# Decoder kernel on one core: later groups' input chain, units, state sums and gated stage under other slots

## What is computed

```python
x = x + _L0_attn_ref(_layernorm(x), ...)            # selective scan
x = x + _L0_xattn_ref(_layernorm(x), ctx_1024, ...) # gated attention over the context, 4 heads
x = x + _L0_ffn_ref(_layernorm(x), ...)             # graph of 6 attention nodes, 8 heads
```

```python
dt = jax.nn.softplus(dt @ dt_proj_w.T + dt_proj_b)
dA = jnp.exp(dt[..., None] * A)
dBu = (dt * u)[..., None] * Bm[:, :, None, :]
def step(h, inp):
    dA_t, dBu_t = inp
    h = dA_t * h + dBu_t
    return (h, h)
y = jnp.einsum('lbin,bln->bli', h_seq, Cm)
y = (y + u * D) * jax.nn.silu(gate)
return y @ out_proj_w.T
```

```python
for c in range(6):
    q = ew[c, 0] * (nodes[in_q] @ We[eq] + be[eq])   # k, v alike from older nodes
    o = _mha(q, k, v, Wq[c], Wk[c], Wv[c], Wo[c])
    nodes[c] = act_w[c] * o + q
```

## Time and profile before

| what | before |
| --- | --- |
| median of 3 runs | 1204.73 us (1203.15 to 1206.0) |
| the profiled execution's own time | 1206.4 us |
| its span (first to last instruction) | 1204.5 us |
| PE matmul busy | 1092.0 us, 91% |
| PE weight loads busy | 840.4 us, 70% |
| DVE busy | 979.9 us, 81% |
| ACT busy | 733.6 us, 61% |
| start of the node graph of group 0 | 194.8 us |

### The profile page before, as it was taken

The page is one execution under the profiler, slowest core; times in us unless marked ns, Lnnn a source line. Parts: engine busy times, 40 slices in busy tenths (PEclk is TensorE's granted clock), DMA queues, the critical chain, the costliest instruction groups (busy, mean ns, idle before and its releaser), DMA issues.

```text
span 1204.5 us, 26893 instructions
## 1 busy us (share of the span) xinstructions
PE 1092.0 (91%) x11428; PEld 840.4 (70%) x11428; DVE 979.9 (81%) x1220; ACT 733.6 (61%) x1728; POOL 15.3 (1%) x33
## 2 busy tenths in 40 slices
PE   8777899999899999999899989999999988998886
PEld 6555577767676777777776767777777766776775
DVE  3799887999989989999899988998998989635122
ACT  4446444776487657766677648765776656544443
POOL 5000000000000000000000000000000000000000
PEclk9778668999999999999999989999999999999998
DMA  7732631041112211041204111221104110000000
GB/s 219 232 114 71 210 106 53 7 136 36 36 37 53 90 45 63 11 133 36 71 7 137 36 31 43 62 81 46 53 11 132 37 62 2 2 1 10 2 2 10
DMA packets 48695, 76.08 MB, mean 63 GB/s; under 512 B 5504, under 2 KB 33408, under 8 KB 48576
## 3 DMA queue, kind: packets, MB, share of 16 engines
q1 hardware_dynamic: 47872, 73.81, 19.4%
q0 software_dynamic: 704, 0.56, 0.2%
HBM read 62.55 MB, written 10.75 MB: 61 GB/s over the span
## 4 chain that ended last, share of the span: by engine, by line
PE 59%; DVE 14%; ACT 7%; issue 5%; DVEq 0%; ACTq 0%
PE ps L651 7%; PE heads L661 6%; PE ps L729 6%; PE heads L682 4%; PE ps L722 4%; PE ps L632 4%; PE heads L690 4%; PE ps L556 4%; DVE ring L1112 3%; DVE mx L1215 3%; PE ps L518 3%; PE ps L579 2%; PE heads L632 1%; PE ps L707 1%; ACT qT L934 1%
## 5 line engine op out<-in xcount | busy, mean ns | idle before, releaser
L1112 DVE TENSOR_TENSOR_SCAN ring<-dec,ring 128x1024 f32<-128x1024 f32 x128 | 292.3, 2283 | 1.0 <-ACT dec L879 0.9
L879 ACT ACTIVATE dec<-dts,a_neg 128x254 f32<-128x254 f32 x512 | 220.3, 501 | 9.9 <-DVE ring L1112 9.8
L1215 DVE TENSOR_REDUCE mx<-heads 128x16 f32<-128x2048 f32 x48 | 109.8, 2288 | 62.9 <-PE heads L682 62.3
L1121 DVE TENSOR_TENSOR ring<-ring,cs 128x1024 f32<-128x1024 f32 x128 | 156.2, 1220 | 2.0
L1105 DVE TENSOR_TENSOR ring<-dtus,bs 128x1024 f32<-128x1024 f32 x128 | 155.4, 1219 | 0.8 <-DVE fb L1026 0.5
L954 ACT ACTIVATE pr<-heads 128x512 f32<-128x512 f32 x192 | 99.1, 602 | 41.9 <-PE heads L695 41.9
L556 PE MATMUL ps<-ring,fold 128*32 128x256 f32 x1024 | 87.7, 412 | 18.6 <-DVE ring L1121 18.3
L729 PE MATMUL ps<-aT,wo_f 128*128 128x256 f32 x384 | 95.0, 388 | 8.2 <-DVE aT L1224 7.9
L722 PE MATMUL ps<-node,we_f 128*128 128x256 f32 x384 | 98.1, 401 | 0.0
L651 PE MATMUL ps<-node,wq_f 128*128 128x256 f32 x384 | 94.9, 390 | 3.4 <-ACT node L969 3.4
L661 PE MATMUL heads<-wv_f,node 128*128 128x256 f32 x384 | 93.3, 386 | 0.0
(11 more groups left out here) (191 smaller groups left out, 1755.2 us busy)
## 6 DMA issues: line engine op xcount, KB each, us to landing
dts<-dt_rows SPq DMA_DIRECT2D x31, 512.0 KB, 4.2
dtus<-dt_rows SPq DMA_DIRECT2D x31, 512.0 KB, 5.1
node<-in_w_edgeT SPq DMA_DIRECT2D x18, 256.0 KB, 3.5
bs<-bc_rows SPq DMA_DIRECT2D x32, 128.0 KB, 4.8
cs<-bc_rows SPq DMA_DIRECT2D x32, 128.0 KB, 4.8
dt_rows<-dt SPq DMA_DIRECT2D x32, 128.0 KB, 2.4
dt_rows<-th SPq DMA_DIRECT2D x32, 128.0 KB, 2.5
xin<-in_x SPq DMA_DIRECT2D x8, 256.0 KB, 3.2
```

The costliest lines, as they stand in the source:

```text
L879: last = fn(dec[k % 2][:, blk, :, 1:L], dts[c % 2][:, blk, :].rearrange("p (b t) -> p b t", b=GB)[:, :, 1:L], ACT.Exp, scale=a_neg[:, c, b ...
L1112: v.tensor_tensor_scan(states, dec[k % 2][:].rearrange("p k b t -> p (k b t)"), states, 0.0, ALU.mult, ALU.add).then_inc(sig["state"], 1)
L1121: v.tensor_tensor(states[:], states[:], cs[:, q:q + 1, :].broadcast_to([P, BLKS, T]), ALU.mult).then_inc(sig["outflow"], 1)
L1215: v.tensor_reduce(mx[:].rearrange("p (h s) -> p h s", h=HPC)[:, :, 0:STEPS], heads[:].rearrange("p h (s k) -> p h s k", s=STEPS), AX.X, AL ...
```

## The change

Every instruction stays. The tables of slots of groups 1 to 7 are others for the input chain, the units and the gated stage, the sums (`add`) leave the unit table for a table of their own, and group 0's steps keep their slots.

```diff
-    if _k >= 1:
-        U_STEPS += [("u", "add", _k - 1)]
-        if _k % CUNITS == 0:
-            U_STEPS += [("u", "gather", _k // CUNITS - 1)]
-U_STEPS += [("u", "weigh", UNITS - 1), ("u", "add", UNITS - 1), ("u", "gather", IC - 1)]
+    if _k >= 1 and _k % CUNITS == 0:
+        U_STEPS += [("u", "gather", _k // CUNITS - 1)]
+U_STEPS += [("u", "weigh", UNITS - 1), ("u", "gather", IC - 1)]
+ADD_STEPS = [("u", "add", k) for k in range(UNITS)]
...
-A_AT = [-101, -70, -68, -67, -65, -64, -62, -59, -56, -45, -42]
...
+A_AT = [-101, -69.5, -68.75, -66.5, -64.5, -63.5, -60.5, -58.25, -55.25, -44.75, -40.75]
...
+ADD_AT = [-25, -23, -16.5, -14, -4, -1.75, 2.75, 9, 10.5, 13, 20, 22.5, 24.75, 28.5, 33.25, 35.25]
...
+X_AT = [34, 37.5, 41.75, 42.75, 45.75, 47.75, 49.5, 51, 54.5, 55.25, 56.75, 57, 57.25, 60.5, 63, 64.75]
...
+FIRST = ((A_STEPS, A0_AT), (U_STEPS, U0_AT), (ADD_STEPS, ADD0_AT), (X0_STEPS, X0_AT))
+LATER = ((A_STEPS, A_AT, A_SH), (U_STEPS, U_AT, U_SH), (ADD_STEPS, ADD_AT, ADD_SH), (X_STEPS, X_AT, X_SH))
```

More of the change, by code:

```diff
@@ L97 @@
 P_STEPS = [("p", "prep", n) for n in range(3 * NODES)]
-A_AT = [-101, -70, -68, -67, -65, -64, -62, -59, -56, -45, -42]
-U_AT = [-44, -40, -40, -39, -34, -34, -32, -32, -32, -32, -32, -32, -32, -29, -29, -29, -25, -25, -25, -25, -24,
[4 rows of a table removed]
-X_AT = [26, 37, 41, 42, 45, 47, 48, 50, 54, 55, 56, 57, 57, 58, 63, 64]
+A0_AT = [-886.25, -822.5, -822, -810.25, -810.25, -810, -804.75, -803.75, -731, -617.25, -601.25]
+A_AT = [-101, -69.5, -68.75, -66.5, -64.5, -63.5, -60.5, -58.25, -55.25, -44.75, -40.75]
+A_SH = [0, -8.25, 1.75, 2, 2, 2, 2, 2]
@@ new lines @@
+U0_AT = [-122, -118, -118, -117, -112, -112, -110, -110, -110, -110, -110, -110, -110, -107, -107, -107, -103,
[4 rows of a table added]
+U_AT = [-42.5, -35.75, -35.25, -35.25, -35.25, -35.25, -32, -31.75, -31.75, -31.75, -31.75, -29.5, -29.25, -28,
[5 rows of a table added]
+U_SH = [0, 1, 1, 1, 1, 1, 1, 1]
+ADD0_AT = [-103, -101, -95, -92, -82, -80, -76, -72, -68, -65, -62, -56, -53, -50, -45, -43]
+ADD_AT = [-25, -23, -16.5, -14, -4, -1.75, 2.75, 9, 10.5, 13, 20, 22.5, 24.75, 28.5, 33.25, 35.25]
+ADD_SH = [0, 1, 1, 1, 1, 1, 1, 1]
+X0_AT = [-38.75, -30.5, -27.5, -22.5, -22, -17.25, -16.75, -16.25, -14, -14, -11, -9.75, -9, -9, -5, -3]
@@ L106 @@
+X_AT = [34, 37.5, 41.75, 42.75, 45.75, 47.75, 49.5, 51, 54.5, 55.25, 56.75, 57, 57.25, 60.5, 63, 64.75]
+X_SH = [0, 1, 1, 1, 1, 1, 1, 1]
 P_AT = [-602.5, -580.75, -567.25, -85.5, -80.75, -78.75, -63.5, -60.75, -57.5, -46.25, -34.5, -31.25, -22.5,
         -20.75, -17.5, -7.25, -2.5, -1]
[L110 to L114, removed]
@@ L115 @@
-AT = (("a", A_STEPS, A_AT, A_SH), ("u", U_STEPS, U_AT, U_SH), ("x", X_STEPS, X_AT, X_SH))
-ORDER = [(FSLOTS * g + n, 0, g, n, step) for g in range(NG) for n, step in enumerate(F_STEPS)]
[L118 to L121, removed]
@@ L122 @@
-ORDER += [(at, 3, 0, n, step) for n, (step, at) in enumerate(zip(X0_STEPS, X0_AT))]
-ORDER += [(at, 4, 0, n, step) for n, (step, at) in enumerate(zip(P_STEPS, P_AT))]
+FIRST = ((A_STEPS, A0_AT), (U_STEPS, U0_AT), (ADD_STEPS, ADD0_AT), (X0_STEPS, X0_AT))
+LATER = ((A_STEPS, A_AT, A_SH), (U_STEPS, U_AT, U_SH), (ADD_STEPS, ADD_AT, ADD_SH), (X_STEPS, X_AT, X_SH))
+ORDER = [(FSLOTS * g + n, 0, g, n, step) for g in range(NG) for n, step in enumerate(F_STEPS)]
+for _rank, (_steps, _at) in enumerate(FIRST):
+    ORDER += [(at, 1 + 2 * _rank, 0, n, step) for n, (step, at) in enumerate(zip(_steps, _at))]
@@ L125 @@
+for _rank, (_steps, _at, _shift) in enumerate(LATER):
+    ORDER += [(FSLOTS * (g - 1) + at + _shift[g], 2 + 2 * _rank, g, n, step)
+              for g in range(1, NG) for n, (step, at) in enumerate(zip(_steps, _at))]
+ORDER += [(at, 9, 0, n, step) for n, (step, at) in enumerate(zip(P_STEPS, P_AT))]
 WARM_FIRST = 10
@@ L128 @@
         -540.25, -537.5, -537.5, -537.5, -524.5, -523, -517, -517, -511.25, -508.25, -508.25, -508.25]
-ORDER += [(at, 5, 0, n, step) for n, (step, at) in enumerate(zip(W_STEPS, W_AT))]
+ORDER += [(at, 10, 0, n, step) for n, (step, at) in enumerate(zip(W_STEPS, W_AT))]
 ORDER = [(step, g) for _, _, g, _, step in sorted(ORDER)]
```

## The result

The changed kernel takes 1191.55 us as the median of 4 runs (1188.22 to 1192.87), the kernel before beside it 1203.94 (4 runs, 1200.33 to 1206.0). The ratio is 0.9896, with a 95% interval of 0.9877 to 0.9914: 12.4 us faster. Five more runs of the changed kernel gave 1191.28, ratio 0.9901 (0.9881 to 0.9922). The forecast was 1199.4, 5.3 us faster, with a range of 1195.3 to 1205.5.

A forecast was written before the change was run, and what follows sets the result against it. Neither TensorE nor VectorE alone was taken as the bound; only changed waits count. Six graphs at -0.79 (-4.7), graph ends -1.7 and group 6 +1.1 gave -5.3, from 1204.73 to 1199.4 us, range 1195.3 to 1205.5.

The forecast's parts named there:

- Node 0, +0.27: Node 0: with the gather between the halves of `aT`, the second half reaches TensorE's output 0.27 us late.
- Start of node 2, +0.43 on TensorE: Node 2's start: decays ahead of `qT` must wait for the scan, so `qT` and TensorE are 0.43 us later.
- Subtraction of node 2: Node 2: `mxT` freed from the decay pair gives -0.79 against +0.43 at the start; the scan replaces VectorE's idle free.
- Transposes -0.49: Context transposes leave the place ahead of node 2's edge product and fit TensorE's 0.66 wait before node 3's scores: -0.49 us.
- halves -0.31: Node 2's output: both halves of `aT` ahead of the weighing remove TensorE's 0.31 us wait before L729's second half.
- First rival: VectorE sets the period and only its gaps count: -0.58 us a graph, 1202.3 in all; chance 0.16.
- End of a graph, -0.34: Graph ends: the sum ahead of the input chain's transposes fills their 0.34 us wait for ScalarE; five graphs, -1.7.
- Graph 6, +1.1: Graph 6: -0.6 in node 0, +2.2 for node 2's uncovered scan, -0.49 for context transposes; together +1.1 us.
- Node 4, +0.10: Node 4: the values' copy ahead of four decays shifts ScalarE's idle before the node's copy; taken as +0.10 us.
- The clock: Rival: gaps gathered in one place bring one more low-clock stretch a graph, 8.6 us, 1208.0, slower; chance 0.08.
- a small gain for one fewer: Larger-gain case: group 3's second low-clock stretch goes (-1.4) and node 0 costs nothing (-1.6): 1196.4; chance 0.10.

The follow-up runs named there:

- gather_back: The changed kernel with node 0's gather ahead of both halves of the product again; median 1190.02 us, ratio 0.9886.
- before_fill: The kernel before with eight unread matmuls ahead of TensorE's wait for the last head's values in node 5; 1201.64 us, ratio 0.9986.
- best: The changed kernel with node 0's gather ahead of both halves for groups 1 to 6, and group 7's maximum ahead of node 2's scan; 1182.26 us, ratio 0.9829.

## Why the prediction was wrong

**Node 0, +0.27: right in sign, measured +0.41.** The second half of `aT` waits behind the gather and nothing brings that back (`gather_back`). VectorE's idle ahead of the first half is 1.62, not 2.0.

**Start of node 2, +0.43 on TensorE: wrong.** The decays did wait for the scan (0.52 of idle) and `qT` is 0.40 later. But the copy of dt had started 0.95 behind `qT`, at 505.32 against 504.37, and now starts 0.71 behind it (370.31, 371.02), which takes up 0.24 of that:

```profile
505.32 0.84 ACT L847 ACTIVATE dt<-ps,vec 128x256 f32<-128x256 f32 x2
```

TensorE's wait grew from 1.01 to 1.17 only.

**Subtraction of node 2: -0.36 forecast, -0.51 measured.** The scan found its cover in groups 0 to 5, as forecast, and had none in graph 6 (+2.17 against 2.2).

**Transposes -0.49 and halves -0.31: the step that failed.** I took each wait of TensorE for a cost of its own. From node 2's maximum to node 3's, VectorE works in graphs 0 to 4 with no other waits than 0.14 and 0.51 in the layer norm, which the change leaves, so those waits of TensorE were only VectorE's delay seen from TensorE. The two edits alone gave +0.32 and +0.07. What the change gained there is VectorE's idle of 1.49, and to that the forecast gave nothing: the scan and the idle were to change places at no cost, and the gain stopped at the subtraction. Over both pieces -1.52 was measured and my sum had -1.16. That the two are near each other is luck: -0.80 of the -1.16 are two terms that don't hold, and the idle was left out.

**First rival.** Its mechanism held in node 2 of graphs 0 to 4 and failed as a rule for the period. Its -1.49 stands against the measured -1.52; the 0.29 that it added between the halves of node 2 didn't come in the change. Its sum of -0.58 a graph assumed that VectorE sets the other nodes too: it had +0.62 in node 0, where +0.41 was measured, and nothing for the end of a graph, where TensorE's order gave -0.73. The Trainium skill, "Perfetto Trace Analysis", "Identifying the Most-Contended Engine", which points to VectorE by its occupancy, agrees with the trace in that stretch, where the time follows VectorE's idle; the shares of the whole window (93% and 72%) could not say in which stretch.

**End of a graph, -0.34: mis-sized, -0.73 measured.** The sum's own move brought 0.46, since it closed VectorE's 0.33 ahead of node 0's maximum too, and for the other 0.27 I had missed the projection between keys and queries.

**Graph 6, +1.1: right,** +1.3 measured, and in its terms too: -0.44 for node 0 (-0.6), +2.17 for the scan (+2.2), -0.39 behind it (-0.49). **Node 4, +0.10:** -0.06.

Of the miss of 0.77 in each of graphs 0 to 4, node 2 makes 0.36, the end of the graph 0.39, node 4 0.16, and node 0 0.14 the other way. By graphs: five graphs at -1.90 and not -1.13 make 3.9 of the miss, graph 5 (-1.39, not -0.79) 0.6, the other way 0.2 in graph 6. That is 4.3 of 7.1 us. The rest, 2.8, is in no term. The profiles show nothing else that differs than the clock and the first part; how the 2.8 divides between them isn't shown.

**The clock.** As a rival I had only more stretches, and a small gain for one fewer. The profile had 9, and I took the profiled execution as typical. At 1206.4 it is 3.5 over the later median of 23 runs (1202.86) and above the slowest of them (1206.34), so fewer stretches were more likely than more.

**Still open.** Why the same wait of 1.36 is followed by a stretch in graph 2 of the change and not in graph 1; and why the first part ends between 208.7 and 211.9 in kernels with the same order there. Every piece was read from one profiled execution of its kernel; that they repeat within 0.02 us from graph to graph is what they rest on.

## What to carry to other kernels

Before adding up the waits of one engine, look whether another works almost without a gap across the same stretch. If it does, its own gaps are the sum and the first engine's waits are one delay, seen several times; an edit that fills one of them then gives nothing, or takes cover away elsewhere. Ask it graph by graph: here graph 5 answered otherwise than graphs 0 to 4. And one profiled execution is one draw: count its low-clock stretches, and compare kernels by distances between fixed points in pieces that have none.

## What the runs showed of the hardware

A wait of 1.36 us of TensorE (573.03 in the earlier trace rows), in a graph of 130.29 us in which its matmuls are busy for 122.44, can be followed by 3.41 us at the granted clock 0.50, its level of 1.2 GHz. Such a stretch makes the graph 1.0 to 1.2 us longer; one at another place 1.6 (before, graph 0: 130.64 against 129.06). Filling the wait with unread matmuls removed the stretches at that place in both orders (in `before_fill` 3 were left of 9, elsewhere). The same wait, of the same length, is not always followed by one. This row of the change is from graph 1, and the clock stays at 1.00 behind it:

```profile
436.99 0.66 PE L627 MATMUL ps<-vaug,ml_buf 128*128 128x65 f32 x4 [1.36 <-DVE ml_buf L1175]
```

In the profile before, graphs 1, 2 and 3 have their stretch at the same place, 129.70 us apart; in that of the change, with shorter graphs, only graphs 2 and 5 have it. So a change that leaves the wait alone still changes how many stretches there are. The runs of one kernel lie 2 to 9 us apart, and in the main a longer run has a lower mean clock: of before, 1206.34 at 0.948 and 1199.31 at 0.955. Not always: the slowest run of `best`, 1185.23, has 0.961, and so has its fastest, 1179.51.
